# Cross-attention with LayerNorm on one core: keyed scores, probabilities and the key bias row in PSUM instead of SBUF

## The reference, cut to what matters

```python
# x: (16, 512, 512) f32   ctx: (16, 120, 256) f32   Wq: 512x512, Wk and Wv: 256x512
q = x @ Wq + bq
k = ctx @ Wk + bk
v = ctx @ Wv + bv
w = einsum('bte,bme->btm', q, k) / sqrt(512)
w = softmax(w, axis=1)              # over the 512 positions t, for each context row m
pred = einsum('btm,bme->bte', w, v)
y = pred + x
out = (y - mean(y)) * rsqrt(var(y) + 1e-6) * gamma + beta
```

## Time and profile before

| | before |
|---|---|
| median of 3 runs | 234.28 us (234.02 to 236.08) |
| profiled execution | 234.56 us |
| its span in the profile | 232.8 us |
| PE, DVE, ACT, POOL busy, share of the span | 83%, 83%, 70%, 73% |
| DMA | 41.04 MB, mean 176 GB/s |

### The profile page before, as it was taken

The page is one execution under the profiler, slowest core; times in us unless marked ns, Lnnn a source line. Parts: engine busy times, 40 slices in busy tenths (PEclk is TensorE's granted clock), DMA queues, the critical chain, the costliest instruction groups (busy, mean ns, idle before and its releaser), DMA issues.

```text
span 232.8 us, 4178 instructions
## 1 busy us (share of the span) xinstructions
PE 193.9 (83%) x1168; PEld 118.6 (51%) x1168; DVE 194.1 (83%) x436; ACT 164.0 (70%) x343; POOL 171.0 (73%) x164
## 2 busy tenths in 40 slices
PE   4788699999899999896998989998989898995100
PEld 4644557474647475554464747474747473542000
DVE  0472875888999997969999998999999999688993
ACT  2525669487878979678797978797979799773510
POOL 1000002269998999999999998999999989894791
PEclk9999999999999999999999999999999999997755
DMA  6999966004545545455455454555554440404044
GB/s 150 297 211 301 355 239 222 3 1 180 203 182 201 184 181 203 182 201 200 181 193 188 184 198 180 201 195 187 187 195 180 180 182 0 183 1 180 0 180 180
DMA packets 11914, 41.04 MB, mean 176 GB/s; under 512 B 1022, under 2 KB 5886, under 8 KB 8062
## 3 DMA queue, kind: packets, MB, share of 16 engines
q1 hardware_dynamic: 11614, 40.37, 49.7%
q10 hardware_dynamic: 288, 0.52, 1.2%
HBM read 24.12 MB, written 16.78 MB: 176 GB/s over the span
## 4 chain that ended last, share of the span: by engine, by line
DVE 24%; issue 22%; POOL 18%; ACT 12%; PE 12%; DMA 7%; DVEq 2%; SPq 1%; POOLq 0%; ACTq 0%
DMA obuf<-in_ctx 7%; DVE xbuf L829 7%; POOL obuf L955 6%; POOL obuf L949 6%; PE s_ps L422 5%; DVE key_junk L762 4%; ACT probs L595 3%; DVE obuf L818 3%; POOL rstd L982 3%; ACT prob_part L601 3%; ACT xT L551 2%; DVE stats L842 2%; POOL v_part L942 2%; PE g_ps L392 2%; DVE prob_part L797 2%
## 5 line engine op out<-in xcount | busy, mean ns | idle before, releaser
L949 POOL TENSOR_TENSOR obuf<-obuf,gamma_all 128x512 f32<-128x512 f32 x44 | 64.7, 1495 | 3.5 <-ACT obuf L614 3.5
L422 PE MATMUL s_ps<-xT,gT 128*120 128x512 f32 x128 | 57.7, 593 | 0.0
L955 POOL TENSOR_TENSOR obuf<-obuf,beta_all 128x1536 f32<-128x1536 f32 (+1 forms) x16 | 52.4, 3275 | 1.2
L414 PE MATMUL pv_ps<-v_part,prob_part 120*128 120x512 f16 x135 | 36.0, 381 | 9.4 <-DVE xbuf L829 4.4
L605 ACT ACTIVATE square_junk<-xbuf,neg_mean 128x512 f32<-128x512 f32 x36 | 25.7, 716 | 18.2 <-DVE neg_mean L837 18.2
L614 ACT ACTIVATE obuf<-xbuf,shift,rstd 128x512 f32<-128x512 f32 x44 | 32.7, 803 | 6.2 <-POOL shift L987 6.0
L422 PEld LDWEIGHTS s_ps<-xT,gT 128*120 128x120 f32 x128 | 23.2, 183 | 26.1 <-issue 19.8
L400 PEld LDWEIGHTS xT_ps<-ident,xbuf 128*128 128x128 f32 x256 | 29.6, 141 | 12.7 <-issue 8.8
L551 ACT ACTIVATE xT<-xT_ps 128x512 f32<-128x512 f32 x64 | 34.2, 585 | 2.2 <-PE xT_ps L400 2.2
L400 PE MATMUL xT_ps<-ident,xbuf 128*128 128x128 f32 x256 | 33.4, 274 | 2.2 <-DMA xbuf<-in_x 1.1
L829 DVE SCALAR_TENSOR_TENSOR xbuf<-pv_ps,back_y,xbuf 128x512 f32<-128x512 f32 x45 | 32.3, 739 | 0.1
(11 more groups left out here) (114 smaller groups left out, 261.8 us busy)
## 6 DMA issues: line engine op xcount, KB each, us to landing
xbuf<-in_x SPq DMA_DIRECT2D x16, 1024.0 KB, 4.8
out<-obuf SPq DMA_DIRECT2D x14, 1024.0 KB, 4.2
out<-obuf SPq DMA_DIRECT2D x8, 256.0 KB, 2.5
ctx_nat<-in_ctx SPq DMA_DIRECT2D x16, 120.0 KB, 4.2
obuf<-in_ctx SPq DMA_DIRECT2D x2, 960.0 KB, 15.2
wq_nat<-in_L_xattn_Wq SPq DMA_DIRECT2D x2, 512.0 KB, 8.9
wk_nat<-in_L_xattn_Wk SPq DMA_DIRECT2D x1, 512.0 KB, 5.8
wv<-in_L_xattn_Wv SPq DMA_DIRECT2D x1, 512.0 KB, 13.9
```

What stands on the lines that cost most here:

```text
L414: mm = pe.matmul(banks[j], prob_part[:, of_p, j * P:(j + 1) * P], v_part[:, k % 2, of_v, :], start=(n == 0), stop=(n == len(PASSES) - 1))
L422: mm = pe.matmul(s_ps[0:M, :], gT[:, k % 2, e, :], xT[:, e, :], start=(e == 0), stop=(e == EC - 1))
L949: pool.tensor_tensor(obuf[:, k % 2, j, :], obuf[:, k % 2, j, :], gamma_all[:], ALU.mult)\
L955: done = pool.tensor_tensor(obuf[:, k % 2, 0:share, :], obuf[:, k % 2, 0:share, :], beta_all[:].unsqueeze(1).broadcast_to([P, share, E]), ...
```

## The change: where three tiles live

The tiles `s_keyed`, `probs` and `w_row` go. `softmax_bias` writes its result back over the scores in `s_ps` (for batch 14 into `g_ps`, because `scores` of batch 15 come early and need `s_ps`); `exponential` works in place there; `probs_to_high` and `probs_to_low` read from there. The key bias row now lies in columns 240 to 496 of `ctx_ps`, where TensorE writes it directly, so the copy of 256 columns out of PSUM goes, and the copy of its last column moves behind TensorE's product. Three waits change: `turn_ctx` waits for the key bias of the batch before (of batch 2 itself in the prologue), since both use the bank `ctx_ps`; `softmax_bias` of batch 14 waits until all copies out of `g_ps` are done; and `scores` of batch 15 wait for `softmax_bias` of batch 14 instead of its exponential.

```diff
-        w_row = sb("w_row", [M, L + 1])
-        probs = sb("probs", [M, T])
-        s_keyed = sb("s_keyed", [M, T])
-        w_ps = v_ps[0:M, 0:L]
+        w_row = ctx_ps[0:M, LC * M:LC * M + L + 1]
...
+        def softmax_bank(b):
+
+            return g_ps if isinstance(b, int) and b == B - 2 else s_ps
...
             def turn_ctx(b, k, r):
                 if is_in(b, 1, B):
                     pe.wait_ge(ctx_low, b)
+                if is_in(b, 2, B):
+                    pe.wait_ge(key_done, max(b, 3) if isinstance(b, int) else b)
...
-                mm = pe.matmul(w_ps[:, c * P:(c + 1) * P], ones[:], w_diag[:, c, :], start=True, stop=True)
+                mm = pe.matmul(w_row[:, c * P:(c + 1) * P], ones[:], w_diag[:, c, :], start=True, stop=True)
...
-                    pe.wait_ge(probs_done, s)
+                    pe.wait_ge(least_done, s)
                     scores(s, k)
...
-                    act.activation(probs[:], s_keyed[:], ACT.Exp, bias=s_least[:], scale=-1.0,
+                    act.activation(softmax_bank(b)[0:M, :], softmax_bank(b)[0:M, :], ACT.Exp, bias=s_least[:], scale=-1.0,
                                    accum_out=s_sum[:]).then_inc(probs_done, 1)
...
-                    act.activation(prob_part[:, HIGH], probs[:], ACT.Copy, scale=s_by[:]).then_inc(prob_high, 1)
+                    act.activation(prob_part[:, HIGH], softmax_bank(b)[0:M, :], ACT.Copy, scale=s_by[:]).then_inc(prob_high, 1)
...
-            dve.tensor_copy(w_row[:, L:L + 1], d_col[0:M, :])
...
             dve.wait_ge(w_spread, 1)
-            dve.tensor_copy(w_row[:, 0:L], w_ps).then_inc(w_row_done, 1)
+            dve.tensor_copy(w_row[:, L:L + 1], d_col[0:M, :]).then_inc(w_row_done, 1)
...
-                dve.scalar_tensor_tensor(key_junk[:, k], ctx_nat[:, k], 1.0, w_row[:], ALU.mult, ALU.mult,
+                dve.scalar_tensor_tensor(key_junk[:, k], ctx_nat[:, k], 1.0, w_row, ALU.mult, ALU.mult,
                                          accum_out=c_key[:, k]).then_inc(key_done, 1)
...
-                    dve.tensor_scalar(s_keyed[:], s_ps[0:M, :], c_key[:, kb], None, ALU.add, ALU.min,
+                    if softmax_bank(b) is g_ps:
+                        dve.wait_ge(g_copied, EC * B)
+                    dve.tensor_scalar(softmax_bank(b)[0:M, :], s_ps[0:M, :], c_key[:, kb], None, ALU.add, ALU.min,
                                       accum_out=s_least[:]).then_inc(least_done, 1)
...
-                    dve.scalar_tensor_tensor(prob_part[:, LOW], probs[:], s_by[:], prob_part[:, HIGH],
+                    dve.scalar_tensor_tensor(prob_part[:, LOW], softmax_bank(b)[0:M, :], s_by[:], prob_part[:, HIGH],
                                              ALU.mult, ALU.subtract).then_inc(prob_low, 1)
```

More of the change, by code:

```diff
@@ L73, in cross_attention @@
     SCALE = float(E) ** -0.5
-    assert T == RJ * P and E == EC * P and L == LC * P and M <= P and EC * M + 1 <= 512
+    assert T == RJ * P and E == EC * P and L == LC * P and M <= P and EC * M + 1 <= 512 and LC * M + L + 1 <= 512
     assert LAST_POOL_J[-TAIL:] == (1, 1) and TAIL == 2 and B % 2 == 0
```

## The result

The changed kernel takes 225.43 us (median of 4 runs, 224.19 to 226.54), the kernel before in the same comparison 235.11 us (4 runs, 234.02 to 236.08). The ratio is 0.9588, with a 95% interval of 0.9504 to 0.9673: 4.1% faster. The prediction was 227.1 us, in a range of 223.0 to 230.0.

What follows compares the result with a forecast made beforehand. VectorE and GpSimd, both nearly full, lengthened each other's instructions; afterwards GpSimd would bound. Loop 4.0 plus tail 3.2, 7.2 us off the profiled 234.56, gives 227.4; the median lies 0.28 lower, so 227.1 us, range 223.0 to 230.0.

Steps and rivals of the forecast that it cites:

- The operands: On VectorE, instructions with two SBUF inputs wait for GpSimd's running one; `probs_to_low` and `key_bias` would become constant, 0.74 to 0.76 and 0.42 us.
- the two stalls: In VectorE's loop slot, waits of `probs_to_low` and `key_bias`, priced at 0.86 and 0.58 us, taking 11.78 to 10.34 us.
- GpSimd becomes the bound, 11.4 us per slot: In the loop, GpSimd's own 10.54 us plus turns of 0.43 and 0.47; 0.31 us less per slot, 4.0 in all.
- The sign that I named: In the loop of the profile after, GpSimd would be busy to 98% or so.
- TensorE's floor of 10.9: In the loop, TensorE's own work per slot, 11.7 less 0.8 us idle, would limit any further gain.
- a rival: In the loop, GpSimd does better than 11.4, down to 10.9 us per slot, 220.3 us in all; chance 0.20.
- The tail, 3.2 us: Behind the loop, TensorE's 3.01 us wait for batch 15's `probs_to_low` goes; gain 2.9 to 3.6 us, 3.2 taken.
- up to 0.6: In the tail, TensorE, no longer left idle for 3 us, may be quicker over the last products.
- a thing that could go wrong: In the tail, the last `center` and `rescale` might collide with GpSimd more than before; no size given.
- The prologue, nothing: Ahead of the loop, the dropped 256-column copy out of PSUM stood before a wait for GpSimd, so no gain.
- The writes into PSUM, nothing: In the softmax, at most 0.1 us less or 0.3 more each for `softmax_bias` and exponential, hidden by 1.1 us of slack.
- The Trainium skill's rule that I weighed: On VectorE, a PSUM source costs 120 fixed cycles, SBUF 58: 0.065 us more each for `probs_to_low` and `key_bias`.

Runs made afterwards that it cites:

- experiment 4: The kernel before, with GpSimd's `plus_beta` of slot 15 split into three instructions of 512 columns instead of one of 1536; 231.23 us, ratio 0.9841.
- experiment 2: The kernel before with only the key bias row moved to PSUM, scores and probabilities still in SBUF; 226.08 us, ratio 0.9632.
- experiment 3: The changed kernel with the probabilities back in an SBUF tile, keyed scores and key bias row still in PSUM; 225.5 us, ratio 0.9608.
- experiment 7: The changed kernel with beta left out for GpSimd's third row group in slots 2 to 15, so less GpSimd work; 216.04 us, ratio 0.9191.
- experiment 8: The changed kernel with a second, unused `key_bias` product per slot on VectorE; 225.11 us, ratio 0.9544.
- experiment 9: The kernel before with the 1028-byte tile `w_row` given the last place in SBUF, so the tiles behind it move; 234.68 us, ratio 0.9958.
- experiments 9 and 10: The second of the pair: the changed kernel with an unused tile in `w_row`'s old place, restoring the old addresses; 226.29 us, ratio 0.962.
- experiments 1 and 2: The two halves alone. The first: only scores and probabilities in PSUM, key bias row in SBUF as in the kernel before; 228.54 us, ratio 0.9753.
- experiment 6: The changed kernel with VectorE's `center` of slot 15 moved behind `probs_to_low` of batch 14; 224.36 us, ratio 0.9551.

## Why the prediction held, step by step

**The operands** (two SBUF inputs wait for GpSimd's instruction): right as a mechanism, by the constant 739 to 752 and 410 to 424 ns and by experiment 4, which leaves the operands as they are and shortens only GpSimd's instruction. But the step put the two stalls down as separate savings, each to be had by its own edit, and that was wrong. Either half alone gives two thirds of the loop's gain, 11.51 and 11.49 us from 11.71, and both give 11.40; either half alone gives all of the tail's (26.9 and 26.5 us, both together 27.2), which the prediction put down to the operand of `probs_to_low`. With the key bias row in PSUM, `probs_to_low` gets through with two SBUF inputs (experiments 2 and 3), because it has moved: it lies beside `rstd` now. That the 0.58 us of `key_bias` is what had pushed it onto `v_part` agrees with the traces but is argued, not shown: I made no kernel that moves it alone.

**GpSimd becomes the bound, 11.4 us per slot**: right, 11.40, and for the reasons given. The slot at 117.94 takes 11.47 us, of which the turns are 0.71 - 0.20 = 0.51 and 0.73 - 0.19 = 0.54; its own work is 10.42. I had 0.43, 0.47 and 10.54, though the turns fall on `square_mean` and `shift` and not on `rstd` and `v_part`. That 11.40 was met to the digit is luck: my sum was 11.44, and the rounding alone is worth 0.5 us in 13 slots. The sign that I named, GpSimd busy to 98%, did not come: it is 141.85 of 148.19 us in the 13 slots, 96%. Experiment 7 (less for GpSimd, 10.53 us a slot) and experiment 8 (more for VectorE, nothing) show that the bound is GpSimd's.

**TensorE's floor of 10.9**: wrong. I took the slot less the two idle gaps as TensorE's own work. With less to do for GpSimd the slot was 10.53 us with the same products. It carried only the end of a rival, so the forecast didn't suffer, but 220.3 was no floor.

**The tail, 3.2 us**: the right mechanism and too small a number; it gave 4.9. TensorE's wait gave 3.0, as worked out. The way from the end of `probs_to_low` to the first `center` behind it is 4.2 instead of 5.0 us; I had allowed up to 0.6 for that and taken 0.2, so another 0.6 is missing there. What I had left out: batch 15's `probs_to_low` starts 6.59 us behind the last loop `rstd` instead of 7.56. That is the other missing 1.0; that it comes of VectorE's and TensorE's chain standing earlier against GpSimd's is argued, not shown. Against it stands the stall of `center` in slot 15, which I had named as a thing that could go wrong.

The 5.0 us of before have a cause of their own. Its last products run at TensorE's lower clock: first before, then before with the row last (experiment 9), where `probs_to_low` stalls just as long.

```profile
212.00:215.00 3.00, 2.93 (x7) 1.04 (x8) 2.39 (x10) 1.60 (x5) 0.40 (x2) 0.51 0.84 350
```

```profile
211.50:213.50 2.00, 1.92 (x9) 0.90 (x10) 1.97 (x8) 1.08 (x3) 0.00 (x0) 1.00 0.92 389
211.59 1.04 PE L414 MATMUL xT_ps<-v_part,prob_part 120*128 120x512 f16 x4 [3.11 <-DVE prob_part L797]
```

TensorE was idle for 3.01 us ahead of the first and for 3.11 us ahead of the second, and only in the first is the granted clock 0.51, close to its lower level of 1.2 GHz; the four products behind the wait take 1.89 us there and 1.04 here. The way to the first `center` is 4.99 us in the first and 3.85 in the second, and the tails are 32.1 and 30.8 us. So of the tail's 4.9 us, 1.3 are due to the clock in the profiled execution of before, and 3.6 are left, the upper end of my 2.9 to 3.6. No other profiled execution has the lower clock in its last products. How many of the unprofiled ones of before have it is not shown; that experiment 4 is 3.2 to 3.3 us below before at either level of time, with a stall only 2.1 us shorter, speaks for most of them.

**The prologue, nothing**: wrong by 1.0 us. By experiments 9 and 10 some 0.6 to 0.8 of it come from where the tiles lie in SBUF, which is no part of the computation; the rest is open. **The writes into PSUM, nothing**: right; VectorE pays 0.07 us a slot, which its slack hides, and the exponential is even at 662 ns beside 722. The Trainium skill's rule that I weighed, 58 against 120 cycles in "VectorE: DVE Perf Modes", in the section on the TRN2 errata, would by the estimate made from it have shown as 0.065 us in both lines: `key_bias` is at 412 against 416 ns and `probs_to_low` at 751 against 744, so there is no such step here.

The sum at one level of the clock (spans 232.8 and 222.8): prologue 1.0, loop 4.1, tail 4.9, together 10.0 us where I had 0, 4.0 and 3.2. The medians give 9.7. The predicted time missed by only 1.7 us, though the gain missed by 2.5, because I had taken 234.28 us for before, which came out at 235.11 in this comparison: 0.8 us of the nearness is luck.

## What to carry to other kernels

Where an instruction's duration varies with its shape fixed, look at what the other engine of the pair runs, and count such stalls as one system: removing one moves the others to another place, for better (experiments 1 and 2) or worse (`center` of slot 15), so that single gains don't add. Before moving small work to the engine with time to spare, ask what runs on its partner at that moment: an instruction of two columns can wait as long as one of 512. And put the bound of a slot to the test by taking work out of one engine at a time; the idle gaps of an engine don't tell how short its slot can be. When two executions differ in the tail, look at TensorE's granted clock there before giving the difference to the change.

## What I had not expected of the hardware

- GpSimd's `rstd` (a power on four columns, 1.02 us) doesn't hold up a VectorE instruction with two SBUF inputs that starts during it: 0.75 us in experiment 2, 0.74 in experiment 6. When it starts during `center`, it does take 1.45. The Trainium skill, "SBUF — State Buffer", in the section with the single rule on contention, has the lock held for a whole instruction; for this one that isn't what the rows show.
- Moving tiles by 1028 bytes in SBUF changed when the first transfers land: `own_bound` starts 0.6 us earlier in one pair of kernels and 0.9 us later in the other.
- Behind 3.01 us without a matmul the granted clock was 0.51 from 212 to 215 us in before; behind 3.11 us in experiment 9 it stayed at 1.00. The first cost 1.3 us in the tail.
- A reduction on VectorE that writes its result into PSUM needs 141 ns to read its accumulator, where 84 was the time with SBUF; ScalarE's exponential in place in PSUM takes 662 ns where it took 722 between SBUF tiles (687 from PSUM to SBUF in experiment 3).
- TensorE's busy time in a slot is 143.8 / 13 = 11.06 us in after (the window from 49.19 to 197.38) and 136.64 / 13 = 10.51 in experiment 7, for the same products: so the profile's busy time of after contains waiting, half a microsecond of it per slot.
